# Macaron block: projection jobs moved to other steps of the attention loop, remainder evictions one step later

## The reference

```python
x = x + 0.5 * ffn(layernorm(x))              # silu(x Wg) * (x Wu), times Wd; hidden 384, int weights / 127
h = silu(layernorm(x) @ W1.T + b1) @ W2.T + b2
q, k, v = split(h @ Wg.T + bg, 3)            # 16 heads of 64
dots = q @ k.T / 8
dots = where(j >= i + 64, -inf, dots)        # row i sees keys 0 .. i + 63
x = x + softmax(dots) @ v @ Wo.T + bo
x = x + 0.5 * ffn(layernorm(x))
```

## Time and profile before

| | |
|---|---|
| median of 3 runs | 1319.61 us (1318.7 to 1322.14) |
| the profiled execution: time, span | 1320.83 us, 1319.1 us |
| PE busy, share of the span | 1264.3 us, 96% |
| POOL busy | 1152.6 us, 87% |
| DVE busy | 936.3 us, 71% |
| ACT busy | 846.4 us, 64% |
| mean granted TensorE clock | 0.994 of full speed |

### The profile page before, as it was taken

One profiled execution on the slowest core, in us unless ns is written; L12 is line 12 of the kernel. 1 busy time (PEld: TensorE's weight loads), 2 busy tenths in 40 slices (PEclk: granted clock), 3 DMA queues, 4 the chain that ended last, 5 costly groups with the idle time before them and its releaser, 6 DMA issues.

```text
span 1319.1 us, 35416 instructions
## 1 busy us (share of the span) xinstructions
PE 1264.3 (96%) x11374; PEld 1003.1 (76%) x11374; DVE 936.3 (71%) x2126; ACT 846.4 (64%) x1898; POOL 1152.6 (87%) x1086
## 2 busy tenths in 40 slices
PE   6988999999999999999999999999999999999988
PEld 5856777777777777877777777777777777777777
DVE  6856777777677777777677777777776776777755
ACT  3655666666666666666666666666666667666642
POOL 6838999999999999999999999999999999999983
PEclk9997999999999999999999999999999999999999
DMA  4242112111121121121111122121111111220001
GB/s 138 85 152 98 43 50 65 65 46 58 65 65 65 65 65 56 34 65 65 56 49 65 65 65 65 65 65 30 60 65 65 41 63 65 65 65 7 8 17 49
DMA packets 80962, 80.22 MB, mean 61 GB/s; under 512 B 38049, under 2 KB 65314, under 8 KB 80930
## 3 DMA queue, kind: packets, MB, share of 16 engines
q1 hardware_dynamic: 80930, 79.82, 18.7%
HBM read 47.13 MB, written 8.39 MB: 42 GB/s over the span
## 4 chain that ended last, share of the span: by engine, by line
PE 68%; issue 13%; DVE 9%; ACT 5%; POOL 1%; SPq 1%; DMA 1%; DVEq 1%; ACTq 0%; POOLq 0%
PE banks L995 18%; PE banks L1012 15%; PE banks L973 15%; PE banks L899 5%; DVE negmax L739 5%; PE banks L953 3%; PE banks L864 3%; PE banks L1017 3%; ACT probs L546 3%; DVE banks L734 2%; PE banks L894 2%; ACT qt L468 2%; PE banks L856 1%; PE banks L857 1%; POOL probs L449 1%
## 5 line engine op out<-in xcount | busy, mean ns | idle before, releaser
L449 POOL TENSOR_SCALAR probs<-probs,recips 128x256 f32<-128x256 f32 (+7 forms) x512 | 881.8, 1725 | 105.9 <-DVE recips L744 105.8
L554 ACT ACTIVATE probst<-banks 128x512 f32<-128x512 f32 (+2 forms) x512 | 266.0, 545 | 276.6 <-PE banks L995 276.6
L546 ACT ACTIVATE probs<-banks,negmax 128x320 f32<-128x320 f32 (+7 forms) x512 | 399.8, 788 | 65.1 <-DVE negmax L739 56.1
L739 DVE TENSOR_REDUCE negmax<-banks 128x1 f32<-128x320 f32 (+7 forms) x512 | 393.9, 811 | 31.9 <-PE banks L973 4.0
L995 PE MATMUL banks<-ident,probs 128*128 128x128 f32 x2304 | 331.2, 280 | 2.0 <-DVE probst L751 1.3
L973 PE MATMUL banks<-kt,qt 64*128 64x512 f32 (+4 forms) x2496 | 303.1, 369 | 29.1 <-ACT probs L546 29.1
L995 PEld LDWEIGHTS banks<-ident,probs 128*128 128x128 f32 x2304 | 250.4, 141 | 82.4 <-issue 74.3
L1012 PE MATMUL banks<-probst,vs 128*64 128x128 f32 (+1 forms) x3328 | 278.2, 317 | 0.1
L973 PEld LDWEIGHTS banks<-kt,qt 64*128 64x128 f32 x2496 | 192.1, 186 | 92.3 <-ACT probs L546 49.1
L1012 PEld LDWEIGHTS banks<-probst,vs 128*64 128x64 f32 x3328 | 201.4, 137 | 72.0 <-issue 22.3
L451 POOL TENSOR_SCALAR ends<-probs,recips 128x64 f32<-128x64 f32 x448 | 198.7, 443 | 0.0
(11 more groups left out here) (72 smaller groups left out, 1040.0 us busy)
## 6 DMA issues: line engine op xcount, KB each, us to landing
xth<-h_split SPq DMA_DIRECT2D x62, 512.0 KB, 4.1
hslot<-h_sb SPq DMA_DIRECT2D x32, 512.0 KB, 3.1
wsplit<-w_split SPq DMA_DIRECT2D x31, 256.0 KB, 4.5
vh<-vs SPq DMA_DIRECT2D x64, 112.0 KB, 2.3
h_split<-qt SPq DMA_DIRECT2D x16, 256.0 KB, 2.2
wslot<-in_wqkvt SPq DMA_DIRECT2D x32, 64.0 KB, 2.5
w_split<-kt SPq DMA_DIRECT2D x4, 512.0 KB, 4.2
y<-xres SPq DMA_DIRECT2D x8, 256.0 KB, 2.3
```

What stands on the lines that cost most here:

```text
L449: last = nc.gpsimd.tensor_scalar(here, here, recips[:, c, h:h + 1], None, ALU.mult)
L546: nc.scalar.activation(probs[c][:, h, :], src, ACT.Exp, bias=negmax[:, c, h:h + 1], accum_out=sums[:, c, h:h + 1]).then_inc(exped.sem, 1)
L554: nc.scalar.activation(probst[c // 2 % 2][:, 4 * g:4 * g + w, c % 2 * P:(c % 2 + 1) * P], banks[:, TRANSPOSED[g % 2], 0:w * P].rearrange(" ...
L739: nc.vector.tensor_reduce(negmax[:, c, h:h + 1], rows[:, h, 0:hi], AX.X, ALU.max, negate=True).then_inc(maxed.sem, 1)
```

## The change

`JOBS` becomes `{0: "v0", 1: "k0", 2: "v1", 3: "k1", 5: "q0", 6: "q1"}`: both value jobs and both key jobs run one step earlier. `q1` keeps step 6, but PE projects it as the last thing in the step, and ACT writes its high part at the beginning of step 7 (`AT_END`). The rests are written a step later on DVE: that of `k0` ahead of the next step's mask (`REST_FIRST`), those of `k1`, `q0`, `q1` behind the next step's row maxima (`REST_LATER`). On ACT the high part of a job in an odd step comes ahead of `attention_out`.

```diff
-    JOBS = {1: "v0", 2: "k0", 3: "v1", 4: "k1", 5: "q0", 6: "q1"}
+    JOBS = {0: "v0", 1: "k0", 2: "v1", 3: "k1", 5: "q0", 6: "q1"}
+    AT_END = {6}
+    REST_FIRST = ("k0",)
+    REST_LATER = ("k1", "q0", "q1")
...
+                if c - 1 in AT_END:
+                    high(JOBS[c - 1])
                 for g in mine:
                     if g < 2:
                         take(tc, g, ti)
                 exps(c, i)
+                if c % 2:
+                    high(JOBS.get(c, "none"))
                 if c in ATTEND_AT and (carry or c >= PV_LAG):
...
                     attention_out(ATTEND_AT[c], i if c >= PV_LAG else i - 1)
-                job = JOBS.get(c, "none")
-                if job[0] in "kq" and runs(job, carry, more):
-                    queries_keys(job, job_turn(job, i), 1 - r if job_turn(job, 0) else r)
+                if c not in AT_END and c % 2 == 0:
+                    high(JOBS.get(c, "none"))
...
+                rest = JOBS.get(c - 1, "none")
+                if rest in REST_FIRST:
+                    evict(rest, i, r, carry, more)
                 row_max(c, i)
+                if rest in REST_LATER:
+                    evict(rest, i, r, carry, more)
                 for g in range(groups[tc]):
                     if turning and taker(tc, g) == 1:
                         take(tc, g, ti)
...
-                if job[0] in "kq":
+                if job[0] in "kq" and job not in REST_FIRST + REST_LATER:
                     evict(job, i, r, carry, more)
...
                 score(c, i, r)
                 if turning:
                     turns_of(tc, ti, (0, 1))
+                if given and c not in AT_END:
+                    run_job()
...
                 if turning and not attending:
                     turns_of(tc, ti, (2, 3))
+                if given and c in AT_END:
+                    run_job()
```

More of the change, by code:

```diff
@@ L567, in step, with high @@
                 mine = [g for g in range(groups[tc]) if turning and taker(tc, g) == 0]
+                def high(job):
+                    if job[0] in "kq" and runs(job, carry, more):
+                        queries_keys(job, job_turn(job, i), 1 - r if job_turn(job, 0) else r)
+                if c - 1 in AT_END:
+                    high(JOBS[c - 1])
                 for g in mine:
@@ L1030, in step, with run_job @@
                 attending = c in ATTEND_AT and (carry or c >= PV_LAG)
-                score(c, i, r)
-                if turning:
-                    turns_of(tc, ti, (0, 1))
                 job = JOBS.get(c, "none")
-                if c in JOBS and runs(job, carry, more):
+                def run_job():
                     k = JOB_ORDER.index(job)
@@ L1043, in step @@
                     project(job, job_turn(job, i), 1 - r if job_turn(job, 0) else r)
+                given = c in JOBS and runs(job, carry, more)
+                score(c, i, r)
+                if turning:
+                    turns_of(tc, ti, (0, 1))
+                if given and c not in AT_END:
+                    run_job()
                 if turning and attending:
```

## The result

| | median | runs | ratio, 95% interval |
|---|---|---|---|
| before | 1319.82 us | 8 | |
| the change | 1324.84 us | 8 | 1.0033 [1.0023, 1.0044] |

The change makes the kernel 0.33% slower, 5.0 us by the medians. The forecast was 14 us slower: the sign is right, the measured step is a third of the forecast one. 1324.84 lies inside the stated range of 1317 to 1343. One of the eight runs of the later experiment `e10_q0_high_first` took 1558 us at a granted clock of 0.75 and is not in its ratio.

What follows compares the result with a forecast made beforehand. PE (busy 96%) was taken as the bound, waiting where the chain comes later: 30 turns at 0.42 us give 12.6, the last turn 1.6, the first 0, sum 14.2 us, hence 1334 us (+1.1%); range 1317 to 1343.

Steps and rivals of the forecast that it cites:

- the sign: Direction of the whole change: slower than the kernel before, 1334 us (+1.1%); slower by more than 4 us got chance 0.73.
- What bounds the kernel: PE, busy 96%, is the engine to follow; differences arise per turn, 30 times, where PE's queue or the chain comes last.
- Step 0 to 1: `v0` and its copy delay the maximum of step 1 by 1.50 us; PE newly waits 0.25, step 2 starts 0.95 late.
- that very case: Bound on the new wait ahead of step 2: nothing if some of the 1.08 us from reciprocal to maximum shrinks.
- Step 1 to 2: Rest of `k0` ahead of the mask of step 2 costs nothing; without cover from ACT's copies, up to 0.3 us.
- Step 2 to 3: Copy of `v1` (0.61) replaces the rest of `k0` (0.66) ahead of step 3's mask; PE released for step 4 at 657.21.
- Step 4: No job left there: 0.70 us less on PE, so step 5 is only 0.39 us late.
- Step 6: `q1` waits about 0.5 us for bank 7 behind the rest of `q0`; step 7's scores come 0.42 later than before.
- Last turn: No key or query job there, so `v0` and `v1` are pure additions ahead of masks: 1.6 us.
- First turn: Late by about one copy at its start, step 4 lighter: 0 in sum.
- per-turn loss: Each turn, from step 0 to step 0, becomes 0.42 us longer; 30 of them give 12.6 us.
- third rival: Only one new wait, step 1's or step 6's, is real: turn 0.17 us longer, 1326 us; chance 0.20.

Runs made afterwards that it cites:

- e10_q0_high_first: The kernel before, with one edit: in step 5 ACT writes the high part of `q0` ahead of `attention_out` instead of behind it; 1313.78 us.
- e1_q0_rest_first: The changed kernel, with the rest of `q0` written ahead of the mask of step 6 again; 1313.93 us, ratio 0.9959 to the kernel before.

## Why the prediction was right or wrong

*What bounds the kernel*: right. Nearly everything happened per turn, in 30 turns, and in the steps where PE waits for the chain.

*Step 0 to 1*: this is the step that failed. "The maximum of step 1 starts at 641.90 + 0.61 + 0.61 + 1.08 = 644.20, 1.50 later than before." On that clock it came 1.18 later. PE shows no named wait ahead of step 2; by the length of step 1, 5.82 us where PE's queue alone gives 5.94 - 0.19 = 5.75, it waited 0.07, not 0.25. Two terms were mis-sized. DVE's copy of the transposes came 0.80 later (3.53 us into the turn, before 2.73) instead of 0.89, since the stretch of step 0 from the output projection on runs 0.14 us shorter with `v0` ahead of it; the run that moves `v0` alone has the same step of 3.42 us. And the 1.08 us from reciprocal to maximum, which I had taken as fixed, shrank to 0.87, while the copy cost the 0.60 that I had given it. I had named that very case as a bound ("nothing if some of the 1.08 us shrinks") and not followed it. Against the forecast step 0 is 0.14 us shorter and step 1 0.18.

*Step 1 to 2*, the rest of `k0` at nothing: held, step 2 took 3.49 as forecast.

*Step 2 to 3*: "the chain keeps its length within 0.05" failed in the same way, and by more. Step 3 took 5.64 us where I had 5.87. From the copy of transposes to the mask the chain is 1.47 us (649.52 to 650.99) and was 1.75; the trade of the rest (0.66) for the copy (0.60) gives only 0.06 of this, and reciprocal to add fell from 0.28 to 0.07. PE's wait there was 0.36 by the row, not 0.5.

*Step 4*: right in kind, 0.09 short.

*Step 6*: right in mechanism, and the only loss there is. The bank came free 4.00 us after the scores of the step began, just as worked out (669.46 - 665.46). The term that was mis-sized is `q1` itself: 0.89 us to the next scores, where I took the 0.70 of the earlier trace rows, in which it lies between other matmuls. It starts on an idle PE here, but no run isolates that: between other groups the timeline has 0.78 to 0.88 us from the start of such a job to the next group. So step 6 took 0.23 more than before, not 0.03.

*Last turn*: 0.83 instead of 1.6. *First turn*: not told apart from the clock.

So the per-turn loss, 0.42 forecast, was 0.16. I had put 0.39 of it ahead of step 6, by way of the copies of values, and 0.03 into step 6; measured it is -0.05 and 0.23. The run without that loss in step 6, `e1_q0_rest_first`, is faster than before. So the sign came out right by a step that carried almost nothing in my sum. My third rival, "only one of the two new waits is real", came nearest, and in the half of it in which step 1 does not wait: it gave 0.17 a turn and 1326. I gave it 0.20. That its number fits so well is partly luck, since it too has 0.14 ahead of step 6 and 0.03 in it, and the two misses cancel.

The rule of the Trainium skill's page "Perfetto Trace Analysis", section "Identifying Performance Opportunities", which sends one to the most contended engine, is borne out only in its subsection "Optimization Strategy" here, which says to look for the gaps on that engine and for what releases them. PE's instructions are the same 11374 in every run, yet the times go from 1299 to 1339 us with the order alone. The section "Matmuls" of the same page has independent groups rotate through PSUM banks, so that one is evicted while the next runs. The trace after agrees in that `q1` waits 0.43 us for the bank that it shares with `q0`. No run gave `q1` a bank of its own, and with the bank still shared the wait is gone once the rest is written early, so here the place of the eviction was enough.

## What to carry to other kernels

When a job is moved on the engine that is the bound, follow its evictions first: here the rest that frees the bank, put behind 1.33 us of other work on DVE (and `q1` at the end of the step), turned a change worth -0.5% into +0.3%. Put an eviction where its engine waits anyway, not where it is "later": two such moves, of work that stayed the same, took the changed kernel from 0.3% slower than the kernel before to 1.6% faster. And the distance between two small instructions is no constant to add up: look for the same pair in other steps of the same trace, and at when the wait ahead of it was met.

## What the hardware showed that I had not expected

On DVE the reciprocal and the add behind it start 0.27 us apart in step 0 of the kernel before (641.62 to 641.89; between them stand one register instruction and two waits of DVE's own sequencer) and 0.08 apart in the changed one. An extra copy ahead of them is not what makes the difference. Step 4 of the kernel before has the pair right behind the copy of transposes too, and there it is 0.07:

```profile
659.33 0.22 ACT L546 ACTIVATION_READ_ACCUMULATOR probs<-banks,negmax 128x1 f32 x1
...
660.09 0.15 DVE L744 RECIPROCAL recips<-sums 128x2 f32<-128x2 f32 x1
660.16 0.40 DVE L769 TENSOR_TENSOR xres<-banks,xres 128x256 f32 x1
```

What goes with it is when ACT ends the exponentials, for which the reciprocal waits. In step 4 their last accumulator read ends 0.54 us before the reciprocal starts; in step 0 of the kernel before it ends 0.16 before (641.24 + 0.22), in that of the changed kernel 1.55 before. By the medians over the turns it holds in every run and every step that has the pair: where the read ends at most 0.13 us before the reciprocal starts, the add follows 0.19 to 0.29 us behind it, and where it ends 0.26 us or more before, 0.07. So `v0` in step 0 shortens the chain because PE brings DVE's copy of transposes later, after the exponentials are done. I read this as DVE's sequencer being held at that wait and taking the small instructions only behind it; a row of the kernel before shows them on the path ("DVEq L766", "DVEq L769"), but no run isolates them, so the reading is argued and not shown. Why step 0 on PE runs 0.14 us shorter with the value job in front of the output projection stays open.
